# Layer 3's dense sums: two products of 32-bit parts for three of bf16

## What is computed

```python
def _rgcn_layer(x, W, SW, b, src, dst, rel):
    xt = jnp.einsum('nd,rde->rne', x, W)
    msg = xt[rel, src]
    agg = jax.ops.segment_sum(msg, dst, num_segments=x.shape[0])
    return jax.nn.relu(agg + x @ SW + b)
...
    x = _rgcn_layer(entity_emb, w1, sl1, b1, src, dst, edge_type)
    x = _rgcn_layer(x, w2, sl2, b2, src, dst, edge_type)
```

## Time and profile before

| | us |
|---|---|
| runs, median of 3 | 1624.51 |
| runs, lowest and highest | 1622.56, 1626.06 |
| profiled execution, span from first to last instruction | 1840.2 |

### The profile page before, as it was taken

The page is one execution under the profiler, slowest core; times in us unless marked ns, Lnnn a source line. Parts: engine busy times, 40 slices in busy tenths (PEclk is TensorE's granted clock), DMA queues, the critical chain, the costliest instruction groups (busy, mean ns, idle before and its releaser), DMA issues.

```text
span 1840.2 us, 25393 instructions
## 1 busy us (share of the span) xinstructions
PE 1562.5 (85%) x9744; PEld 949.8 (52%) x9744; DVE 779.7 (42%) x2390; ACT 520.8 (28%) x749; POOL 917.4 (50%) x931
## 2 busy tenths in 40 slices
PE   1379989998578889988899787898888998889986
PEld 1365554444355556555565455554555655556545
DVE  7999961337345555555465654530010010001102
ACT  0464520015234435444354543420000000000000
POOL 6500000000566566666666665646666666666665
PEclk9999999999789899999899998998999999989988
DMA  4312331534443444544455443325555355555441
GB/s 124 103 73 90 127 162 72 195 129 185 155 141 134 151 156 165 189 163 159 151 182 179 157 157 122 113 82 189 186 192 189 123 190 188 190 189 178 172 148 47
DMA packets 67473, 275.85 MB, mean 150 GB/s; under 512 B 19988, under 2 KB 25854, under 8 KB 54676
## 3 DMA queue, kind: packets, MB, share of 16 engines
q1 hardware_dynamic: 37940, 213.87, 30.1%
q0 software_dynamic: 29408, 60.29, 12.1%
HBM read 153.70 MB, written 120.38 MB: 149 GB/s over the span
## 4 chain that ended last, share of the span: by engine, by line
PE 66%; DVE 14%; another core or an unknown queue 6%; issue 6%; DMA 3%; POOL 2%; ACT 2%; POOLq 0%; DVEq 0%; ACTq 0%
PE ps L1385 34%; DVE hot_mem L1667 8%; PE ps L1408 8%; PE ps L1263 7%; PE ps L1297 7%; PE ps L1449 2%; PE ps L1435 2%; PE ps L1306 2%; ACT blocks L929 2%; DMA node_id<-table_rel,edges 1%; POOL node_id L798 1%; DMA acc<-table_rel,edges 1%; DVE hot_mem L1812 1%; POOL acc L798 1%
## 5 line engine op out<-in xcount | busy, mean ns | idle before, releaser
L798 POOL DMA_INDIRECT node_id<-table_rel,edges x445 | 439.0, 987 | 608.0 <-DMA table_rel<-node_id 358.3
L798 POOL DMA_INDIRECT acc<-table_rel,edges x429 | 419.3, 977 | 257.5 <-issue 113.2
L1385 PE MATMUL ps<-blocks,raw 128*128 128x512 f16 x1500 | 456.5, 393 | 15.5 <-DVE xn L1917 12.5
L929 ACT ACTIVATE blocks<-ps 128x800 f16<-128x800 f32 x384 | 315.6, 836 | 342.3 <-PE ps L1297 200.0
L1385 PE MATMUL ps<-blocks,dinv 128*128 128x512 f16 x1200 | 399.3, 395 | 13.5 <-issue 12.8
L1809 DVE TENSOR_SCALAR hot_mem<-cell_h,rel_cols 128x128 f16<-128x128 f16 x768 | 165.6, 268 | 265.9 <-PE ps L1297 152.9
L1297 PE MATMUL ps<-hot_mem 128*128 128x400 f16 x768 | 198.8, 344 | 68.0 <-ACT blocks L929 47.5
L1408 PEld LDWEIGHTS ps<-raw,node_id 128*128 128x128 f32 x996 | 193.8, 200 | 97.7 <-issue 38.9
L1385 PE MATMUL ps<-blocks,edges 128*128 128x512 f16 x600 | 236.8, 395 | 7.9 <-issue 7.6
L1408 PEld LDWEIGHTS ps<-raw,acc 128*128 128x128 f32 x962 | 183.7, 197 | 85.4 <-issue 31.0
L1812 DVE TENSOR_SCALAR hot_mem<-cell_h,rel_cols 128x400 f16<-128x400 f16 x768 | 224.8, 333 | 0.0
(11 more groups left out here) (183 smaller groups left out, 1296.2 us busy)
## 6 DMA issues: line engine op xcount, KB each, us to landing
rcounts<-blocks SPq DMA_DIRECT2D x44, 1600.0 KB
blocks<-rcounts SPq DMA_DIRECT2D x44, 1600.0 KB
counts<-blocks SPq DMA_DIRECT2D x6, 3200.0 KB, 11.0
blocks<-counts SPq DMA_DIRECT2D x5, 3200.0 KB, 10.5
table_rel<-node_id SPq DMA_DIRECT2D x50, 256.0 KB, 2.1
table_rel<-xn SPq DMA_DIRECT2D x50, 256.0 KB
node_id<-table_rel,edges POOLq DMA_INDIRECT x445
acc<-table_rel,edges POOLq DMA_INDIRECT x429
```

The lines of the kernel that those rows point to most:

```text
L798: nc.gpsimd.indirect_dma_start(got[m % GATHERS][:, j, :], None, tables_rel[layer - 2], bass.IndirectOffsetOnAxis(ap=row_i[:, first + j:fir ...
L929: nc.scalar.activation(to.rearrange("p t (b m) -> p t b m", b=2), ps[:, strip_bank(k):strip_bank(k) + 2, 0:RCELLS].rearrange("p b (m t) -> ...
L1385: last = nc.tensor.matmul(ps[:, bank, 0:2 * HCOLS], part, half_pairs[u % 2][:, :, t * HCOLS:(t + 1) * HCOLS], start=(k == 0), stop=(k == T ...
```

## The change

Layer 3's features are stored as two 32-bit parts instead of three bf16 ones. The type is float32r: stored in 32 bits, with fewer bits of mantissa kept than f32 has. ScalarE's copy out of PSUM to that type is the high part (`high_tile`), VectorE's subtraction the low one (`low_tile`); the middle part and its two operations go. A product takes both operands in this type, so the counts too must be in it. ScalarE and VectorE copy them, tile by tile in turn (`widen_until`, casts of 128 x 512 from f16), into a ring of 12 tiles (`conv_mem`), at most 10 ahead of the slot. The ring lies over memory of layer 2's one-hots (`hot_mem`) and over a part of `raw`; the parts lie over `dinv`, `edges`, `raw` and in one new buffer. A pair now takes 25 steps of two products (L1443, L1444; `sum_tile`), 1200 products in all. A step waits for its cast, a cast waits for the step 12 before it. `load_pair` waits until the pair two before has been cast instead of summed, and GpSimd's gates count steps (`tile_summed`) instead of quarters.

```diff
+CONV = 12
+AHEAD_CONV = CONV - 2
...
-    n, pairs, sums = TILES * PARTS, MADE // 2, []
+    n, pairs, sums = TILES, MADE // 2, []
...
+        def wait_to_widen(eng, i, first):
+
+            if first:
+                eng.wait_ge(half_summed, PAIRS2)
+                eng.wait_ge(rstrip_copied, MADE * HSTRIPS)
+            u = i // TILES
+            if u >= 2 and (i % TILES) < 2:
+                for r in (2 * (u % 2), 2 * (u % 2) + 1):
+                    eng.wait_ge(halves_loaded[r], 16 * (u // 2))
+            if i >= CONV:
+                eng.wait_ge(tile_summed, i - CONV + 1)
...
             def load_pair(p):
-                sp.wait_ge(half_summed, PAIRS2 + p - 1)
+                sp.wait_ge(act_wide, (TILES * (p - 1) + 1) // 2)
+                sp.wait_ge(dve_wide, TILES * (p - 1) // 2)
...
-                                    pool.wait_ge(quarter_summed, 4 * (n - AHEAD) + j // 2 + 1)
+                                    steps = steps_until[n - AHEAD + 1] - steps_until[n - AHEAD]
+                                    pool.wait_ge(tile_summed, steps_until[n - AHEAD] + steps * (j // 2 + 1) // 4)
...
+                def high_tile(r, bank):
+                    act.wait_ge(tile_turned, r + 1)
+                    nc.scalar.activation(high3(row_order[r]), ps[:, bank, 0:P], ACT.Copy).then_inc(tile_high, 1)
...
+                def sum_tile(u, k):
...
+                    i, t = u * TILES + k, row_order[k]
+                    pe.wait_ge(*wide(i))
+                    nc.tensor.matmul(ps[:, u % 2, 0:2 * HCOLS], high3(t), wide_tile(i), start=(k == 0), stop=False)
+                    nc.tensor.matmul(ps[:, u % 2, 0:2 * HCOLS], low3(t), wide_tile(i), start=False, stop=(k == TILES - 1)).then_inc(tile_summed, 1)
...
+                def low_tile(r, bank):
                     t = row_order[r]
                     dve.wait_ge(tile_high, r + 1)
-                    nc.vector.tensor_tensor(rest3[:, r % 2, :], ps[:, bank, 0:P], parts3[0][:, t * D:(t + 1) * D], ALU.subtract)\
-                        .then_inc(tile_rest, 1)
...
+                    nc.vector.tensor_tensor(low3(t), ps[:, bank, 0:P], high3(t).bitcast(f32), ALU.subtract).then_inc(tile_low, 1)
+
+                widened = [0]
+
+                def widen_until(end):
+                    for i in range(widened[0], min(end, STEPS3)):
+                        if i % 2:
+                            wait_to_widen(dve, i, i == 1)
+                            nc.vector.tensor_copy(wide_tile(i).rearrange("p (h n) -> p h n", h=2), narrow_tile(i)).then_inc(dve_wide, 1)
+                    widened[0] = max(widened[0], end)
...
                     for s in range(slots3):
                         if s + 1 < slots3:
                             node_onehots(3, s + 1)
+                        widen_until(steps_until[s + 1] + AHEAD_CONV)
```

More of the change, by code:

```diff
@@ L227, in gnn_kernel, with sb_over @@
     with ExitStack() as stack:
+        place = {}
         def sb(name, shape, dt=f32):
+            place[name] = nc.sbuf_base
             return stack.enter_context(nc.sbuf_tensor(name, shape, dt))
+        def sb_over(name, shape, dt, under, at=0):
+            return nc.alloc_sbuf_tensor_at(name, shape, dt, offset=-(-place[under] // 32) * 32 + at)
         def sem(name):
@@ L552, in sums_done, with sums3_done, wide, wide_tile @@
             return [w for w, _, end in pieces if end == TILES * PARTS]
+        steps_until = [TILES + sum(b - a for t in range(s) for _, a, b in sums3[t]) for s in range(slots3 + 1)]
+        STEPS3 = TILES * (MADE // 2)
+        assert steps_until[-1] == STEPS3
+        def sums3_done(s):
+            return [w for w, _, end in sums3[s] if end == TILES]
+        def wide(i):
+            return (dve_wide if i % 2 else act_wide), i // 2 + 1
+        def wide_tile(i):
+            return conv_mem[i % CONV // (CONV // 2)][:, i % (CONV // 2), :]
+        def narrow_tile(i):
+            u, t = i // TILES, row_order[i % TILES]
+            return half_pairs[u % 2][:, :, t * HCOLS:(t + 1) * HCOLS]
+        def high3(t):
+            return high3_mem[:, t, :]
+        def low3(t):
+            if t < LOW_TILES[0]:
+                return low3_mem[0][:, t, :]
+            t -= LOW_TILES[0]
+            return low3_mem[1][:, t, :] if t < LOW_TILES[1] else low3_mem[2][:, t - LOW_TILES[1], :]
+        def wait_to_widen(eng, i, first):
[8 more added lines that the diff above has]
+                eng.wait_ge(tile_summed, i - CONV + 1)
         def blocks_done(layer, s):
@@ L675, in relational @@
                 for s in range(slots3 + 2):
-                    while s < slots3 and 2 * at < MADE and at * TILES * PARTS <= sum(b - a for t in range(s + 1) for _, a, b in sums3[t]):
+                    while s < slots3 and 2 * at < MADE and at * TILES <= sum(b - a for t in range(s + 1) for _, a, b in sums3[t]):
                         if at + 2 < MADE // 2:
@@ L1413, in add_message, with sum_and_add @@
                         last.then_inc(batch_done, 1)
-                def sum_and_add(layer, s, products_, first, end, sums_of=None):
+                def sum_and_add(layer, s, products_, first, end):
                     messages = len(gathers[layer].in_slot[s])
-                    quarters = [len(products_) * q // 4 - 1 for q in range(1, 5)] if layer == 3 and products_ else []
-                    quarters = [i - (products_[i][1] == TILES * PARTS - 1) for i in quarters]
                     for i in range(first, end):
-                        sum_product(sums_of or layer, *products_[i], i in quarters)
+                        (sum_product if layer == 2 else sum_tile)(*products_[i])
                         for message in range(messages * i // len(products_), messages * (i + 1) // len(products_)):
@@ L1474, in relational @@
                             if turned:
-                                pe.wait_ge(tile_rest, turned)
+                                pe.wait_ge(tile_low, turned)
                             end_quad(2, i)
@@ L1496, in relational @@
                             row_products(r, h, TAIL_BANKS[2 * n + h])
-                    for k in range(TILES * PARTS):
-                        sum_product(3, 0, k)
+                    for k in range(TILES):
+                        sum_tile(0, k)
                     for s in range(slots3 + 1):
@@ L2013, in relational @@
                             node_onehots(3, s + 1)
+                        widen_until(steps_until[s + 1] + AHEAD_CONV)
+                        if s == first_final + 1:
+                            for u in range(STAGES3):
+                                dve.wait_ge(stored3[u], 16 * len(range(u, 2 * TILES, STAGES3)))
                         for f in finals_of(s - 1):
```

111 lines of the change are left out of this document (45 added, 66 removed).

## The result

The changed kernel takes 1634.4 us (median; 1631.5 to 1637.4), the kernel before 1624.1 in the same runs: ratio 1.006, 95% interval 1.0044 to 1.0076. It is **10 us slower** where 23 us less were forecast; the range 1545 to 1645 holds the time. The kernel before takes 1624 to 1626 us in some series of runs and 1830 to 1850 in others, and its profile ahead of the prediction is from an execution of the long kind, while the changed kernel's profile is of the short kind (span 1631.4). So the two can't be laid side by side; the profile of before that answers to that of after is the one of the first experiment, with a span of 1622.6 us. I call it "before, again".

A forecast was written before the change was run, and what follows sets the result against it. Layer 3 was taken as bound by TensorE and GpSimd within some per cent of each other. 545 us would become 522 + 12 = 534 (-11), with -12 for a shorter pitch: 1624.5 - 23 = 1601.5, about 1600 us; range 1545 to 1645.

The forecast's parts named there:

- the start of the sum: Layer 3 before the change, undisturbed: 614 us profiled less 69 us of "issue" on the chain, about 545 us.
- the floor itself: GpSimd's least time for layer 3: 4.2 + 505 (404 gathers at 1.25 us) + 13.2 = 522 us.
- GpSimd's pitch of 1.22 us: Layer 3's gathers, 1.25 us apart in the profile, taken as 1.22 us apart undisturbed: -12 us more.
- The gathers beside casts: VectorE's casts lengthen layer 3's 405 gathers by 0.030 us each: +12 us, from 0 to +68.
- Rival B: VectorE's casts lock out GpSimd's gathers; decides from 24 us, about 1655 us at +68; chance 0.12.
- The products: Layer 3 on TensorE: 600 of 1800 products go, the 1200 left cost 0.216 us each: -130 us of its work.
- Rival C: TensorE's 32-bit products slower than 16-bit, deciding from 0.33 us each: about 1720 us at 0.43, over 2100 at 0.86; chance 0.09.
- A: Whole saving: stalls also in undisturbed runs, or GpSimd's pitch 1.1 there; 70 to 90 us go, 1535 to 1555; chance 0.13.
- The copies: 600 casts at 0.6 us on ScalarE and 0.5 on VectorE, covered by the ring: 0 on the path.
- GpSimd takes over, TensorE waits at the messages: Layer 3 slots: GpSimd 10.0 us, TensorE 7.2, waiting 2 to 3 us before most slots' first message; 1560 to 1618, chance 0.62.
- Rival D: Nothing moves: floor of 522 us plus 11 to 20 of interference against 545; about 1621 to 1626 us; chance 0.04.

The follow-up runs named there:

- the first experiment: The kernel before, unchanged, run once more for a second profiled execution: 1624.5 us, span 1622.6 us.
- the casts moved: The changed kernel with all 600 casts on ScalarE, 1621.2 us (0.9974 of before), or all on VectorE, 1652.0 us (1.0165).
- the half-gather kernels: The kernel before and the changed kernel, each with every second gather of layer 3 left out: 1716.1 and 1632.9 us, where the full kernel before took 1830.4.

## Why the prediction was wrong

**The step that failed is the start of the sum**: "layer 3 of an undisturbed run then takes about 614 - 69 = 545 us". It takes 529. I struck only TensorE's "issue" time from an execution of the long kind, and left in it GpSimd's idle time, which I read as two engines that hold each other up. It belongs to the long execution: GpSimd's 107 + 117 us of idle time are 63 + 77 in a short one. The very pause of 2.89 us that I quoted as a wait for products was none: the product that this gather's semaphore counts to had ended 6.2 us before the gather began. With 600 products taken away and nothing else changed the kernel takes 0.9997 of its time: one runner set the pace, not two. The sign that I had and didn't use was the floor itself: 522 us for GpSimd with 0.30 of pause in each step, in an execution 13% longer than the runs. With 529 for the 545, the sum of the prediction, without the 12 us for a shorter pitch (below), reads 529 before and 534 after: slower by 5 us, against 8 measured. The 16 us here and the 12 there are 28 of the 33 us between -23 and +10. Of the 534 the floor of 522 measured 519.3 (2.1 + 504 + 13.2), and the lengthening 18.2 for 12: the +12 was put on a floor of bare gathers, which lacks the 5.9 that the kernel before has already. That the first gather came 2.6 us sooner in the changed kernel's profile isn't shown to be the change's: with the casts moved it came 1.1 and 0.1 sooner.

**GpSimd's pitch of 1.22 us** was wrong. It is 0.944 + 0.304 = 1.248 in every execution, short and long. The -12 us taken for it had no row; the 0.30 of "issue" belongs to each gather.

**The gathers beside casts**: +12 us forecast, 12.3 measured. The same rule gives 24 for 600 casts, where 33.2 - 5.9 = 27.3 were measured. The size was right, but the rule has no mechanism in it: the lengthening isn't spread over the gathers by VectorE's busy share, 336 of 405 took under 0.95 us and 35 hold 15.3 of the 18.2 us. That it came so close is in part luck. As forecast, the gathers' mean is 0.99 us. Rival B is this mechanism. Its price is 12 us and not the 24 from which I let it decide, since the gain that it had to beat was not there.

**The products**: 0.230 us for 0.216, 1200 x 0.014 = 17 us. After a message the first product pair costs about 0.07 us more than with bf16 (0.398 us from the message to the second product, for 0.328), 450 x 0.07 = 31 us. Together 48, and -130 becomes -84 as the half-gather kernels show: 130 - 84 = 46. None of it reached the end of the program. Rival C didn't come, and nor did A: the saving of 70 to 90 us exists, but only where half the gathers are gone. The f32 rows of four times the price were no guide to this type.

**The copies** cost 0.63 us on ScalarE and 0.44 to 0.46 on VectorE (0.6 and 0.5 forecast) and held up TensorE once, 1.3 us at the start. VectorE waited for room in the ring, 174.7 + 84.5 us, so the price of 0 on TensorE's path was right:

```profile
L1998 DVE CAST conv_raw<-blocks 128x512 fp32r<-128x512 f16 x150 | 68.2, 456 | 86.3 <-PE ps L1444 84.5
L1998 DVE CAST conv_hots<-blocks 128x512 fp32r<-128x512 f16 x149 | 64.9, 441 | 174.8 <-PE ps L1444 174.7
```

**GpSimd takes over, TensorE waits at the messages**: right, 77.7 us of waits, except that GpSimd had nothing to take over. Rival D, nothing moves, is nearly what comes with the casts on ScalarE (0.9974), but not for its reason, 11 to 20 us of interference that eat the gain: the gathers' lengthening is 5.1 us there.

## What to carry over

Before a stall is struck from one engine's account, look for its like on every other engine; an execution 13% longer than the runs says nothing of which engine is the bound, but 404 steps of a constant 1.248 us do. Then ask whether the relieved engine is that one, by an experiment that only takes work away (600 products less: 0.9997). When work is put on an engine beside the one that sets the pace, choose one that doesn't disturb it: in a short series 600 casts cost 31 us more on VectorE than on ScalarE.

## What the runs showed of the hardware

- A GpSimd gather of 128 rows of f32 took 0.944 us and the next came 0.304 us later, with 1800 products of layer 3 for TensorE as with 1200.
- A gather begun amid VectorE casts without a pause took 6.88 us and ended 0.46 us after the last of them, another took 7.12; two others amid such casts took 1.11 and 1.09. In the changed kernel 171 of 210 beside casts alone took under 0.95. The one-hots of two stored operands lengthened the gathers as well (1060 ns beside them); with one stored operand it was 956. The same casts on ScalarE lengthened no gather.
- float32r products of 512 columns followed each other every 0.230 us, bf16 every 0.216. After a message the first two took about 0.07 us more with float32r than with bf16.
- The same kernel took 1624 us in one series and 1830 or 1850 in another, at a clock nearly the same (0.986 for 0.953). In the long ones GpSimd pauses for about 3 us at waits whose products had ended long before. With half of layer 3's gathers TensorE's weight loads paused for over 0.6 us only 3 times up to the last 15 us of a long execution, and 54 times with all of them (11 in a short one); in layer 2, whose gathers were all there, they paused 68 times in that same execution (21 in a short one). So the disturbance goes with the gathers. Why is open.
